# A decoder layer on one core: the final norm loads each block of rows by its own count of additions, and VectorE normalises five of the sixteen blocks

## The reference

```python
logits = x @ gate_w
scores = softmax(logits); topk_w, topk_idx = top_k(scores, 2)
g = silu(einsum('td,edh->teh', x, w_gate)) * einsum('td,edh->teh', x, w_up)
routed = einsum('teh,ehd,te->td', g, w_down, comb)
shared = silu(x @ sw_gate) * (x @ sw_up) @ sw_down
x = layernorm(x + routed + shared)
```

## Time and profile before

| | us |
|---|---|
| three runs | 1102.69, 1105.0, 1107.13 (median 1105.0) |
| profiled execution, its own time | 1105.46 |
| its span, first to last instruction | 1103.7 |
| PE busy | 958.9 (87%) |
| DVE busy | 756.6 (69%) |
| ACT busy | 608.9 (55%) |
| POOL busy | 463.0 (42%) |

### The profile page before, as it was taken

One profiled execution on the slowest core, in us unless ns is written; L12 is line 12 of the kernel. 1 busy time (PEld: TensorE's weight loads), 2 busy tenths in 40 slices (PEclk: granted clock), 3 DMA queues, 4 the chain that ended last, 5 costly groups with the idle time before them and its releaser, 6 DMA issues. The chain is left out here.

```text
span 1103.7 us, 17998 instructions
## 1 busy us (share of the span) xinstructions
PE 958.9 (87%) x5111; PEld 712.2 (65%) x5111; DVE 756.6 (69%) x1313; ACT 608.9 (55%) x918; POOL 463.0 (42%) x423
## 2 busy tenths in 40 slices
PE   5999999699999999945999999982879999999960
PEld 4556787344444444324889898872868888888850
DVE  3323655777777777418888888843867889888844
ACT  3433211477676776724444444432766888888844
POOL 2000000265555655656565656523233545555423
PEclk9999999799999999966999999995998999999985
DMA  7454700543342442033111111134794434444338
GB/s 249 153 191 161 238 22 1 115 115 90 82 114 66 105 99 73 1 101 114 56 51 58 58 57 57 49 108 146 251 283 78 70 69 74 76 70 73 68 46 306
DMA packets 80881, 115.71 MB, mean 105 GB/s; under 512 B 15680, under 2 KB 37056, under 8 KB 80832
## 3 DMA queue, kind: packets, MB, share of 16 engines
q1 hardware_dynamic: 66320, 90.69, 27.6%
q0 software_dynamic: 9760, 20.49, 10.1%
q10 hardware_dynamic: 4752, 3.94, 1.2%
HBM read 74.77 MB, written 40.31 MB: 104 GB/s over the span
## 5 line engine op out<-in xcount | busy, mean ns | idle before, releaser
L1759 DVE TENSOR_TENSOR we_lo<-w_all,we_hi 128x1408 fp32r<-128x1408 f32 (+1 forms) x117 | 189.1, 1666 | 31.4 <-ACT we_hi L1692 22.3
L612 POOL TENSOR_TENSOR pair_sum<-probs 128x2048 f32<-128x2048 f32 x32 | 146.4, 4575 | 96.6 <-ACT probs L756 96.6
L784 DVE TENSOR_REDUCE maxima<-ps_s 128x8 f32<-128x512 f32 x240 | 150.7, 685 | 51.9 <-PE ps_s L640 51.1
L1692 ACT ACTIVATE we_hi<-w_all 128x1408 fp32r (+1 forms) x117 | 161.5, 1413 | 37.3 <-PE e_ps_y L1818 19.8
L756 ACT ACTIVATE probs<-ps_st 128x512 f32<-128x512 f32 x256 | 143.1, 597 | 69.3 <-PE ps_st L695 65.6
L1663 POOL DMA_INDIRECT x_dram<-e_y,who x39 | 63.6, 1632 | 136.0 <-ACT e_y L1709 120.3
L1657 POOL DMA_INDIRECT xg<-x_dram,who x39 | 74.2, 1902 | 41.7 <-DMA who<-table_dram 24.6
L1448 PE MATMUL ps_gu<-sw_hi,x2T_hi 128*128 128x352 f32 (+1 forms) x256 | 88.2, 345 | 1.9 <-issue 1.5
L1448 PE MATMUL ps_gu<-sw_hi,x2T_lo 128*128 128x352 f32 (+1 forms) x256 | 84.1, 328 | 0.0
L1448 PE MATMUL ps_gu<-sw_lo,x2T_hi 128*128 128x352 f32 (+1 forms) x256 | 83.9, 328 | 0.0
L598 POOL MEMSET ones_sum<- 128x32 f32 x1 | 0.1, 125 | 186.8 <-POOLq L52 186.8
(11 more groups left out here) (251 smaller groups left out, 2493.0 us busy)
## 6 DMA issues: line engine op xcount, KB each, us to landing
qk_dram<-qk_ctx SPq DMA_DIRECT2D x32, 512.0 KB, 2.8
q_more<-qk_dram SPq DMA_DIRECT2D x60, 128.0 KB, 3.0
k_more<-qk_dram SPq DMA_DIRECT2D x60, 128.0 KB, 3.2
w_all<-in_L_ffn_w_gate_dram SPq DMA_DIRECT2D x8, 704.0 KB
w_all<-in_L_ffn_w_up_dram SPq DMA_DIRECT2D x8, 704.0 KB
q_first<-qk_dram SPq DMA_DIRECT2D x36, 128.0 KB, 3.0
k_first<-qk_dram SPq DMA_DIRECT2D x36, 128.0 KB, 3.2
x_dram<-x SPq DMA_DIRECT2D x16, 256.0 KB, 2.0
```

Of the source, the lines that this page charges most:

```text
L612: pool.tensor_tensor(pair_sum[:, h], probs[:, 2 * h], probs[:, 2 * h + 1], ALU.add).then_inc(added, 1)
L784: dve.tensor_reduce(by_tile[:, t, j, 1:9], bank(p, x).rearrange("p (g n) -> p g n", n=S // 8), axis=AX.X, op=ALU.max).then_inc(s_reduced, 1)
L1692: act.activation(w_hi[kind][:], raw(base, kind), ACT.Copy).then_inc(s[kinds[kind] + "_hi"], 1)
L1759: dve.tensor_tensor(w_lo[kind][:], raw(base, kind), w_hi[kind][:].bitcast(F32), ALU.subtract).then_inc(s[kinds[kind] + "_lo"], 1)
```

## The change

Three things, all about the final norm.

First, the last wait is split by block of rows. All tiles of experts 0 to 6 come before those of the last expert, so block n has all its additions once those tiles are through and so many tiles of the last expert as hold tokens of blocks 0 to n. Stage 4 therefore keeps, after each block, the column of the last expert of `both_sum` (`so_far`); a second matmul of ones sums it over the partitions; `plan` copies the result and the number of the others' tiles; and VectorE works out, at the head of `experts`, the number of additions that each block needs (`adds_needed`). SP waits for 32 additions (the least that there can be), reads the number of each block into a register, waits for it and issues the load. All sixteen loads are SP's now, ScalarE's queue has none.

Second, POOL takes the statistics in groups of 2, 2, 4, 4 and 4 blocks, not in eight pairs, and does not wait for the last addition any more; it writes the constant -0.5 at the head of the stage.

Third, ScalarE normalises blocks 0 to 10 and VectorE, behind its statistics, blocks 11 to 15. SP's stores stay in order of the blocks.

```diff
@@ plan_memory, plan
+    t.ps_so_far = ps_xT[:, E:E + NT]
-    dve.tensor_copy(t.at, t.at_i)
+    dve.tensor_copy(c.tile_start[:], t.at_i)
...
     dve.tensor_scalar(c.expert_of[:], t.e_of[0:1, :], float(E - 1), None, ALU.min)
+    dve.tensor_copy(c.so_far_count[:], t.ps_so_far[0:1, :])
+    dve.tensor_copy(c.others_end[:], t.end[0:1, E - 2:E - 1])
@@ cross_and_shared, locate (VectorE) and the end of TensorE
                     step(dve.tensor_tensor(both_sum[:], both_sum[:], both[:], ALU.add))
+                    dve.tensor_copy(c.so_far[:, bass.ds(n, 1)], both_sum[:, E - 1:E]).then_inc(s["so_far_done"], 1)
...
-                pe.matmul(plan_tiles.ps_count, ones[:], both_sum[:], start=True, stop=True).then_inc(s["plan_counted"], 1)
+                pe.wait_ge(s["so_far_done"], NT)
+                pe.matmul(plan_tiles.ps_count, ones[:], both_sum[:], start=True, stop=True)
+                pe.matmul(plan_tiles.ps_so_far, ones[:], c.so_far[:], start=True, stop=True).then_inc(s["plan_counted"], 1)
@@ experts
-        half = m.sb("half3", [P, 2])
+        half = m.sb("half3", [P, 4])
+        groups = [slice(a, z) for a, z in ((0, 2), (2, 4), (4, 8), (8, 12), (12, NT))]
+        DVE_ROWS = range(NT - 5, NT)
@@ SP
-                sp.wait_ge(s["y_added"], 16 * NJ)
-                for n in range(0, NT, 2):
+                sp.wait_ge(s["y_added"], 16 * (2 * T // P))
+                sp.wait_ge(needed_done, 1)
+                for n in range(NT):
+                    adds = sp.value_load(adds_needed[0:1, n:n + 1], min_val=16 * NT, max_val=16 * NJ)
+                    sp.wait_ge(s["y_added"], adds)
                     sp.dma_start(x3[:, n, :], x3_rows[:, n, :]).then_inc(x3_in[n], 16)
                 for n in range(NT):
-                    sp.wait_ge(o_done, n + 1)
+                    if n in DVE_ROWS:
+                        sp.wait_ge(o_dve_done, n - DVE_ROWS.start + 1)
+                    else:
+                        sp.wait_ge(o_done, n + 1)
                     sp.dma_start(out_rows[:, n, :], o[:, n, :]).then_inc(o_out, 16)
+                sp.wait_ge(s["y_added"], 16 * NJ)
                 sp.wait_ge(o_out, 16 * NT)
@@ POOL
                 pool.memset(g[:], 0.0).then_inc(s["padded"], 1)
+                pool.memset(half[:], -0.5).then_inc(half_done, 1)
...
                     if j == 1:
                         pool.wait_ge(s["padded"], 1)
+                        pool.wait_ge(half_done, 1)
...
-                pool.wait_ge(s["y_added"], 16 * NJ)
-                pool.memset(half[:], -0.5).then_inc(half_done, 1)
                 pool.wait_ge(half_done, 1)
-                for q in range(NT // 2):
-                    pair = slice(2 * q, 2 * q + 2)
-                    wait_apart(pool, mv_done, 2 * q + 2, c.pool_passed)
+                for q, group in enumerate(groups):
+                    wait_apart(pool, mv_done, group.stop, c.pool_passed)
...
@@ ScalarE
-                act.wait_ge(s["y_added"], 16 * NJ)
-                for n in range(1, NT, 2):
-                    act.dma_start(x3[:, n, :], x3_rows[:, n, :]).then_inc(x3_in[n], 16)
-                for n in range(NT):
-                    act.wait_ge(bias_done, n // 2 + 1)
+                for n in range(DVE_ROWS.start):
+                    act.wait_ge(bias_done, group_of(n) + 1)
@@ VectorE
+                def adds_before(last_rows, starts):
+
+                    dve.tensor_tensor(begun, last_rows, starts, ALU.is_gt).then_inc(begun_done, 1)
+                    dve.wait_ge(begun_done, 1)
+                    dve.tensor_reduce(begun_tiles[:], begun, axis=AX.X, op=ALU.add).then_inc(begun_done, 1)
+                    dve.wait_ge(begun_done, 2)
+                    dve.tensor_scalar(adds_needed[:], begun_tiles[:], c.others_end[0:1, 0:1], 16.0, ALU.add, ALU.mult).then_inc(needed_done, 1)
...
                     dve.bn_aggr(mv[:, n, :], stats[:, n, :]).then_inc(mv_done, 1)
+                for n in DVE_ROWS:
+                    dve.wait_ge(bias_done, group_of(n) + 1)
+                    dve.tensor_scalar(o[:, n, :], x3[:, n, :], rstd[:, n:n + 1], nbias[:, n:n + 1], ALU.mult, ALU.add).then_inc(o_dve_done, 1)
```

More of the change, by code:

```diff
@@ L856, in plan_memory @@
     t.count, t.length, t.end = take(E), take(E), take(E)
-    t.e_of, t.start, t.row, t.tile, t.at = take(NJ), take(NJ), take(NJ), take(NJ), take(NT)
+    t.e_of, t.start, t.row, t.tile = take(NJ), take(NJ), take(NJ), take(NJ)
     t.at_i, t.tile_i = m.sb("at_i", [P, NT], I32)[:], m.sb("tile_i", [P, NJ], I32)[:]
     t.ps_count = ps_xT[:, 0:E]
+    t.ps_so_far = ps_xT[:, E:E + NT]
     return t
@@ L1004, in cross_and_shared @@
                  "x2_turned hi_done2 lo_done2 r_max r_e r_step rank_done slots_done scat token_done "
-                 "g_done u_done silu_done g_ready gT_turned gT_hi_done gT_lo_done y_done y_out both_done x3_st plan_built plan_counted plan_step").split()
+                 "g_done u_done silu_done g_ready gT_turned gT_hi_done gT_lo_done y_done y_out both_done x3_st plan_built plan_counted plan_step so_far_done").split()
         s = {k: m.sem("p4_" + k) for k in names}
@@ L1573, in experts, with group_of @@
         nbias = m.sb("nbias3", [P, NT])
-        half = m.sb("half3", [P, 2])
+        half = m.sb("half3", [P, 4])
+        groups = [slice(a, z) for a, z in ((0, 2), (2, 4), (4, 8), (8, 12), (12, NT))]
+        DVE_ROWS = range(NT - 5, NT)
+        def group_of(n):
+            return next(q for q, group in enumerate(groups) if n < group.stop)
+        begun = y[0:1, 0, 0:NT * NT].rearrange("p (n i) -> p n i", i=NT)
+        begun_tiles = m.sb("begun_tiles", [1, NT])
+        adds_needed = m.sb("adds_needed", [1, NT], I32)
+        begun_done, needed_done = m.sem("begun_done"), m.sem("needed_done")
         x3_in = [m.sem(f"x3_in{n}") for n in range(NT)]
@@ L1674, in _ @@
                         scatter(j - XG, j % 2)
-                pool.wait_ge(s["y_added"], 16 * NJ)
-                pool.memset(half[:], -0.5).then_inc(half_done, 1)
                 pool.wait_ge(half_done, 1)
-                for q in range(NT // 2):
-                    pair = slice(2 * q, 2 * q + 2)
-                    wait_apart(pool, mv_done, 2 * q + 2, c.pool_passed)
-                    pool.tensor_scalar(ve[:, pair], mv[:, pair, 1], EPS, None, ALU.add).then_inc(ve_done, 1)
-                    pool.tensor_scalar(minus[:, pair], mv[:, pair, 0], -1.0, None, ALU.mult).then_inc(minus_done, 1)
+                for q, group in enumerate(groups):
+                    wait_apart(pool, mv_done, group.stop, c.pool_passed)
+                    pool.tensor_scalar(ve[:, group], mv[:, group, 1], EPS, None, ALU.add).then_inc(ve_done, 1)
+                    pool.tensor_scalar(minus[:, group], mv[:, group, 0], -1.0, None, ALU.mult).then_inc(minus_done, 1)
                     pool.wait_ge(ve_done, q + 1)
-                    pool.tensor_tensor(rstd[:, pair], ve[:, pair], half[:], ALU.pow).then_inc(rstd_done, 1)
+                    pool.tensor_tensor(rstd[:, group], ve[:, group], half[:, 0:group.stop - group.start], ALU.pow).then_inc(rstd_done, 1)
                     pool.wait_ge(minus_done, q + 1)
                     pool.wait_ge(rstd_done, q + 1)
-                    pool.tensor_tensor(nbias[:, pair], minus[:, pair], rstd[:, pair], ALU.mult).then_inc(bias_done, 1)
+                    pool.tensor_tensor(nbias[:, group], minus[:, group], rstd[:, group], ALU.mult).then_inc(bias_done, 1)
             @block.scalar
@@ L1884, in decoder @@
         c.expert_of = m.sb("expert_of", [1, NJ], I32)
+        c.so_far = m.sb("so_far", [P, NT], BF16)
+        c.so_far_count = m.sb("so_far_count", [1, NT])
+        c.tile_start = m.sb("tile_start", [P, NT])
+        c.others_end = m.sb("others_end", [1, 1])
         c.w_in = m.sem("w_in")
```

6 lines of the change are left out of this document (4 added, 2 removed).

## The result

The changed kernel takes 1093.76 us (median of six runs, 1092.8 to 1095.65) against 1104.57 for the kernel before (six runs, 1101.03 to 1107.13): a ratio of 0.9899, 95% interval 0.9882 to 0.9916. That is 10.8 us less. The prediction was 1095.3 with a range of 1092 to 1100, and its sum was 9.7 less.

What follows compares the result with a forecast made beforehand. POOL's chain of pairs and the DMA traffic of loads and stores were taken to bound the tail. Span 1103.7 to 1093.7, plus 0.3 in front, made 9.7 us less: 1095.3 against the median, range 1092 to 1100.

Steps and rivals of the forecast that it cites:

- When the loads start: Final norm's loads: blocks 0 to 10 need 35 additions, the rest 36; sixteen loads from 1050.8 to 1068, 1.1 us apart.
- rival 4: Loads before the norm: every block needs all 39 additions, loads start at 1077.1, time about 1110; chance 0.03.
- VectorE's statistics: Final norm: VectorE starts its means and variances at 1066.99, takes 11.2 us as before, ends at 1078.2.
- Cost 0 to 2, taken as 0, since it lands 1.5 us early as it is: Last tiles: loads sharing the DMA engines with scatters could land the 38th scatter 2.2 us later, counted as no cost.
- rival 3: Last tiles: additions and loads delay scatters and instruction fetch, 3 to 5 us go back, time 1099; chance 0.10.
- Behind it 6.25 as before, so 1093.2: End of the span: 6.25 us pass after the last store's issue at 1086.9, as in the kernel before.
- the 0.55 for the engines' backlog: End of the span: stores of blocks 8 to 15 need 5.2 us on the DMA engines, ending 0.55 later, at 1093.7.
- POOL's chain: Final norm: first group at 1074.1, a group of four 1.92 us, last bias at 1083.1; chain 9.0 instead of 12.9.
- Rival 1: POOL's groups in the norm: a group of four costs twice a pair, 3.24 us, time 1097.1; chance 0.08.
- Behind the last bias: End of the norm: the last store follows the last bias after 3.8 us, where it was 1.6 before.
- The front: Work added ahead of the tail, such as the copy per block and second matmul: 0 to 0.5 us, taken as 0.3.
- Rival 2: Stage 4: the 16 copies wait for POOL, 1.16 us each, and delay TensorE by 18.6 us, to 1113.9; chance 0.03.

Runs made afterwards that it cites:

- the kernel with the front alone: Kernel before plus all that the change adds ahead of the tail, final norm as before, against the kernel before: 1104.48 us, ratio 0.9994.

## Why the prediction was right, and where its steps were not

- **When the loads start** was right: the counts of 35 and 36 additions, and the first load 4.87 us behind the issue of the 35th scatter (1043.98 to 1048.85), where 4.83 was forecast. A read and an issue took 0.92 to 0.99 us, taken as 1.1. No load was waited for. So rival 4 (all 39 additions needed) is excluded.
- **VectorE's statistics** took 10.8 us from start to end against 11.2.
- **"Cost 0 to 2, taken as 0, since it lands 1.5 us early as it is"** is the step that failed. It put 2.2 more us on the 38th scatter alone. The size was about right, the place was not: the loads held up the 37th (7.54 to land, 2.7 more than 4.8), the 38th waited for it and the 39th for the 38th, which made the last scatter 2.9 us later behind ScalarE's last y and 2.4 later behind `g_low`. That is half of rival 3, which had 3 to 5 us for it; the time is better than that rival because of this smaller size and of the next point. The other half of rival 3, slower tiles, is not there: from the issue of the 35th scatter to the end of `g_low` it takes 21.05 us after and 21.02 before.
- **"Behind it 6.25 as before, so 1093.2"** and the 0.55 for the engines' backlog also failed. The 6.25 of the kernel before was no property of a store: POOL's drain of 6.69 us ended 1.2 us behind SP, and the stores landed slowly (4.5 us at the median before, 2.1 after). Of the 6.25, 3.65 pass from the last issue to SP's drain and 1.2 are the wait for POOL's; in the changed kernel SP's drain is 2.97 behind the last issue and waits for nobody. So 4.37 is left, 2.4 less than the 6.8 that the sum had: 1.2 the drain, 0.7 the landing, and 0.55 the backlog, of which there is no sign. That the stores land later because loads' traffic is ahead of them fits the other kernels (3.4 to 4.7 us where the last loads are late, 2.0 to 2.1 where they are early); it was not varied by itself.
- **POOL's chain**: a group of four at 1.99 against 1.92, five groups in 9.2 against 9.0. The power on four columns took 1.04 where 0.57 and 0.72 had given 1.02. Rival 1 (3.24) is excluded.
- **Behind the last bias** the last store follows 3.88 later (3.8). VectorE's five blocks and ScalarE's eleven did as forecast.
- **The front**: taken as 0.3. The changed kernel issues its first list 0.4 later than the kernel before, but that time differs from 754.1 to 757.5 over the profiles of this study, and the kernel with the front alone shows no cost. Rival 2 (the copies reach TensorE) is excluded by the copy's 156 to 160 ns. The rule of the Trainium skill, page "SBUF — State Buffer", section "Who interferes with whom", by which a VectorE copy in a mode with two ports and a POOL instruction exclude one another, changed nothing here: in 9 of 16 cases POOL's L1124 was running and the copy was no longer for it. Whether a copy of one element uses such a mode, no run shows.
- **Signs that failed**: the last store 6.3 to 7 before the end (4.37), and the last scatter. It was issued at 1072.72, ahead of the 1073 that was to be a sign of an error, and POOL's first group at 1074.34 where 1074 was forecast, only because this execution came to its tail 2 us earlier; behind `g_low` both are over 2 us late.

Counted from `g_low`, the sum had the last scatter at 5.3, the first group at 7.1, the last bias at 16.1, the last store at 19.9 and the end at 26.7; measured are 7.7, 9.3, 18.5, 22.4 and 26.8. The end is right by luck: two errors of about 2.4 us, each in a step of its own, cancel. What is shown of the gain, by the medians: without early loads the rest of the change loses 3.9 us; early loads alone gain 5.8 (1098.12 against 1103.95 of the same group). By single profiles: with pairs in place of the groups of four the tail is 3.7 longer, 2.9 of it because POOL's drain starts, and so ends, later, and 0.8 by SP's later stores; VectorE's blocks add at most 0.8. So the groups of four pay mainly by letting POOL's drain start earlier: where earlier drains shorten it, pairs come level, though helped by a last scatter that was 1.2 to 1.9 us less late than in the two profiles of the changed kernel.

## What to carry to other kernels

Before a time behind the last store is carried over to a changed kernel, look at the drains of the barrier: which engine's ended last, and when did it start? In the changed kernel POOL's ends only 0.4 us ahead of SP's, so that earlier stores alone could gain no more than that. Splitting a last wait into counts pays where the consumer idles, but what it releases early runs beside the chain that was the bound, and a serial chain of small transfers pays for every bulk load among its packets. Moving loads off that chain gains nothing where the same loads are needed just behind it.

## What the runs showed of the hardware

- POOL's drain at the end of a stage with 78 indirect DMAs takes 6.69 to 6.70 us in every profile that has no earlier drain, with pairs or groups; 0.53 and 0.79 where an earlier drain leaves 3 and 6 indirect DMAs behind it. At the end of stage 4, behind 32, it is 2.68. A drain just behind a scatter takes 5.2 to 6.6.
- The packets of an accumulating scatter, 144, run for 2.2 to 2.4 us alone and 2.8 to 4.8 with a stream of 256 KB loads beside them (windows of 0.1 us). From issue to landing it takes 4.5 to 5.4 us alone, 4.8 in most cases, and 6.0 to 7.6 beside loads. Three loads were enough for 6.9.
- Stores of 256 KB that follow no loads land in 2.0 to 2.1 us at the median, against 3.4 to 4.7 in the kernels whose last loads are late.
- A read of a number into a register, a wait against it and the issue of a load came 0.92 to 0.99 us apart on SP; issues alone 0.51.
